# A graph attention layer on one core: the exponentials' transposes move from TensorE matmuls to VectorE 32x32 blocks and SBUF transfers, with attention three row blocks behind

## What is computed

```python
h = maximum(layernorm(x), 0)
q, k, v = h @ Wq + bq, h @ Wk + bk, h @ Wv + bv
adj = zeros((N, N)).at[src, dst].set(1.0)
a = q @ k.T / sqrt(512)
a = a * adj + (1 - adj) * -1e6
x = x + softmax(a, axis=-1) @ v
h = maximum(layernorm(x), 0)
agg = segment_sum(h[src], dst) / maximum(segment_sum(1, dst), 1)[:, None]
x = x + alpha * (agg @ W.T + b)
```

## Time and profile before

| what | value |
|---|---|
| median of three runs | 236.05 us |
| the profiled execution's own time | 235.76 us |
| its span in the profile | 233.9 us |
| TensorE busy | 230.2 us (98%) |
| VectorE busy | 161.5 us (69%) |
| ScalarE busy | 81.5 us (35%) |
| POOL busy | 76.0 us (32%) |
| granted TensorE clock | full speed (1.00) |

### The profile page before, as it was taken

One profiled execution on the slowest core, in us unless ns is written; L12 is line 12 of the kernel. 1 busy time (PEld: TensorE's weight loads), 2 busy tenths in 40 slices (PEclk: granted clock), 3 DMA queues, 4 the chain that ended last, 5 costly groups with the idle time before them and its releaser, 6 DMA issues.

```text
span 233.9 us, 3310 instructions
## 1 busy us (share of the span) xinstructions
PE 230.2 (98%) x1290; PEld 188.1 (80%) x1290; DVE 161.5 (69%) x282; ACT 81.5 (35%) x151; POOL 76.0 (32%) x106
## 2 busy tenths in 40 slices
PE   8999999999999999999999999999999999999995
PEld 6476788988888888888888888888888888888884
DVE  5998999999989755884759975757574262073222
ACT  3589927725114140431442341424242002060000
POOL 4386126510000059950702570706064206000000
PEclk9999999999999999999999999999999999999999
DMA  6999101000000020040000000000000000001232
GB/s 193 353 387 403 60 3 46 0 3 0 0 3 0 0 92 3 3 179 0 0 0 3 0 0 0 3 0 1 0 0 3 0 0 0 3 3 45 110 114 90
DMA packets 7152, 12.30 MB, mean 53 GB/s; under 512 B 1120, under 2 KB 2144, under 8 KB 7008
## 3 DMA queue, kind: packets, MB, share of 16 engines
q1 hardware_dynamic: 6272, 11.67, 13.8%
q10 hardware_dynamic: 864, 0.40, 0.6%
HBM read 9.97 MB, written 2.10 MB: 52 GB/s over the span
## 4 chain that ended last, share of the span: by engine, by line
PE 98%; DVE 0%; issue 0%; POOL 0%; DVEq 0%; POOLq 0%
PE bank L832 19%; PE bank L821 16%; PE bank L823 16%; PE bank L822 16%; PE bank L989 12%; PE bank L848 8%; PE bank L905 3%; PE bank L1009 3%; PE bank L898 3%; PE bank L882 1%; PE bank L816 1%; PE bank L892 1%; DVE o_sb L803 0%; PE bank L855 0%; PE bank L871 0%
## 5 line engine op out<-in xcount | busy, mean ns | idle before, releaser
L446 ACT ACTIVATE h2f<-xs,nmr,rstd 128x512 f32<-128x512 f32 x8 | 6.5, 816 | 56.1 <-POOL nmr L385 56.1
L821 PE MATMUL bank<-V_hi,pT_hi 128*128 128x512 f32 x64 | 25.5, 399 | 0.0
L577 DVE TENSOR_TENSOR ohW<-iotaW,key_b 128x1280 bf16<-128x1280 bf16 (+4 forms) x33 | 25.2, 764 | 0.0
L821 PE MATMUL bank<-hT_hi,GT_hi 128*128 128x512 f32 x64 | 25.1, 392 | 0.0
L573 DVE TENSOR_TENSOR ohL<-iotaL,lo_b 128x1024 bf16<-128x1024 bf16 x33 | 22.7, 687 | 3.5 <-PE bank L848 3.4
L823 PE MATMUL bank<-hT_hi,GT_lo 128*128 128x512 f32 x64 | 24.9, 390 | 0.0
L822 PE MATMUL bank<-V_lo,pT_hi 128*128 128x512 f32 x64 | 24.9, 390 | 0.0
L823 PE MATMUL bank<-V_hi,pT_lo 128*128 128x512 f32 x64 | 24.9, 390 | 0.0
L822 PE MATMUL bank<-hT_lo,GT_hi 128*128 128x512 f32 x64 | 24.9, 389 | 0.0
L989 PE MATMUL bank<-A,h_hi 128*128 128x512 f32 x64 | 24.9, 389 | 0.0
L989 PE MATMUL bank<-A,h_lo 128*128 128x512 f32 x64 | 24.9, 389 | 0.0
(11 more groups left out here) (133 smaller groups left out, 497.0 us busy)
## 6 DMA issues: line engine op xcount, KB each, us to landing
xs<-in_x SPq DMA_DIRECT2D x4, 512.0 KB, 8.0
out_dram<-o_sb SPq DMA_DIRECT2D x7, 256.0 KB, 2.0
wv_raw<-in_wv SPq DMA_DIRECT2D x1, 1024.0 KB, 11.4
wk_rows<-in_wk SPq DMA_DIRECT2D x1, 1024.0 KB, 12.8
wq_rows<-in_wq SPq DMA_DIRECT2D x1, 1024.0 KB, 11.7
wt_raw<-in_wT SPq DMA_DIRECT2D x1, 1024.0 KB, 5.1
wq_raw<-in_wqT SPq DMA_DIRECT2D x3, 256.0 KB, 7.7
wk_raw<-in_wkT SPq DMA_DIRECT2D x3, 256.0 KB, 7.6
```

The source lines that it names most:

```text
L577: nc.vector.tensor_tensor(ohW[:, q % RING, :, 0:row].rearrange("p b (m two) -> p b m two", two=2), bcast(iotaW[:, 0:row].rearrange("p (m t ...
L821: mm(out, lhs[0][a], rhs[0][b], start=(first and k == 0), stop=False)
```

## The change

- The 64 transposes on TensorE are gone. VectorE turns each of the 32 blocks of 32x32 of pr's row block in place in one instruction, `nc.vector.transpose`, into a new tile `turned` (128 x 1024). The block that stands in rows a and block column b then has to go to rows b: SP moves it with 16 transfers for each row block, each 32 partitions with 1 KB in each, from `turned` to `pT_f`. Both tiles have two buffers.
- pT_hi is one ScalarE copy of 1024 columns from pT_f in SBUF (it was two of 512 from PSUM), and pT_lo one VectorE subtraction of 1024 columns with both inputs in SBUF. Both walk quarter by quarter (`by_quarter`).
- The attention of a block, its residual, its second norm and POOL's work for it follow three row blocks behind the scores, not two. ScalarE's pT_hi and VectorE's pT_lo are for block i-2 in step i.
- POOL's fill waits for VectorE's transpose, not for TensorE's.
- wt lies where `turned` and `pT_f` lie, so SP loads it after the last pT_lo, and wt_hi and wt_lo are made in the last step (i = 10), no longer in i = 3; on VectorE `wt_lo` now stands ahead of the degrees and of the last residual.

The diff:

```diff
--- before.py
+++ after.py
@@ -196,8 +196,12 @@
         M = [place("M_hi", [P, KD, D], F32R, r_W2), place("M_lo", [P, KD, D], F32R, r_W2 + 8 * KB)]
 
         pr = [place(f"pr{i}", [P, N], F32, r_W0 + 4 * KB * i) for i in range(2)]
+        Q = 32
+        NQ = P // Q
+        pT_f = [place(f"pT_f{i}", [P, NQ, NT, Q], F32, r_W1 + (8 + 4 * i) * KB) for i in range(2)]
         pT = [[place(f"pT_hi{i}", [P, NT, P], F32R, r_W0 + (8 + 8 * i) * KB),
                place(f"pT_lo{i}", [P, NT, P], F32R, r_W0 + (12 + 8 * i) * KB)] for i in range(2)]
+        turned = [place(f"turned{i}", [P, NQ, NT, Q], F32, r_W1 + 4 * i * KB) for i in range(2)]
         h2f = [place(f"h2f{i}", [P, D], F32, r_W0 + (24 + 2 * i) * KB) for i in range(2)]
         r_st = [place(f"r_st{i}", [P, HALF], F32R, r_W0 + (24 + 2 * i) * KB) for i in range(2)]
         b_sb = place("b_sb", [P, D], F32, r_W0 + 28 * KB)
@@ -276,7 +280,8 @@
         gen_prep, gen_iota, gen_stage, gen_deg, gen_cols = (sem(n) for n in ("gen_prep", "gen_iota", "gen_stage", "gen_deg", "gen_cols"))
         agg_stage, agg_used = sem("agg_stage"), sem("agg_used")
         filled, scored, masked, maxed, expd = (sem(n) for n in ("filled", "scored", "masked", "maxed", "expd"))
-        pT_ps, pT_hi, pT_lo = sem("pT_ps"), sem("pT_hi"), sem("pT_lo")
+        blocks_turned, pT_hi, pT_lo = sem("blocks_turned"), sem("pT_hi"), sem("pT_lo")
+        pT_in = [sem(f"pT_in{i}") for i in range(2)]
         attended, x2_ready, h2_hi, h2_lo, res2_ready = (sem(n) for n in ("attended", "x2_ready", "h2_hi", "h2_lo", "res2_ready"))
         agg_ps, agg_hi, agg_lo = sem("agg_ps"), sem("agg_hi"), sem("agg_lo")
         rdeg_ready, out_ps, out_ready = sem("rdeg_ready"), sem("out_ps"), sem("out_ready")
@@ -288,6 +293,10 @@
         def bcast(ap, dim, n):
 
             return ap.unsqueeze(dim).broadcast_to([*ap.shape[:dim], n, *ap.shape[dim:]])
+
+        def by_quarter(tile):
+
+            return tile[:, :, :].rearrange("p t (b c) -> p b t c", b=NQ)
 
         def score_bank(i, q):
 
@@ -333,8 +342,15 @@
             sp.dma_start(bv_sb[:, :], bv_d.partition_broadcast(P)).then_inc(ld_bv, 16)
             sp.wait_ge(proj, NPROJ)
             sp.dma_start(b_sb[:, :], b_d.partition_broadcast(P)).then_inc(ld_b, 16)
-            sp.wait_ge(counts_final, 1)
-            sp.wait_ge(res_ready, NT)
+            for j in range(NT):
+                sp.wait_ge(blocks_turned, j + 1)
+                if j >= 2:
+                    sp.wait_ge(pT_lo, j - 1)
+                for a in range(NQ):
+                    for b in range(NQ):
+                        sp.dma_start(pT_f[j % 2][b * Q:(b + 1) * Q, a, :, :],
+                                     turned[j % 2][a * Q:(a + 1) * Q, b, :, :]).then_inc(pT_in[j % 2], 16)
+            sp.wait_ge(pT_lo, NT)
             sp.dma_start(wt_raw[:, :, :], wT_d.rearrange("(k p) n -> p k n", p=P)).then_inc(ld_wt, 16)
             for n, (j, cols) in enumerate(OUT):
                 sp.wait_ge(out_ready, n + 1)
@@ -403,7 +419,7 @@
             def fill(i):
 
                 if i >= 2:
-                    pool.wait_ge(pT_ps, 2 * (i - 1))
+                    pool.wait_ge(blocks_turned, i - 1)
                 else:
                     link(nc.gpsimd.memset(pr[i][:, :], 0.0))
                 nc.gpsimd.tensor_scalar(pr[i % 2][:, :], pr[i % 2][:, :], 0.0, negc[:, i:i + 1],
@@ -418,16 +434,16 @@
                 add_bv(t)
             pool.wait_ge(ld_b, 32)
             link(nc.gpsimd.tensor_scalar(b_sb[:, :], b_sb[:, :], alpha[:, :], None, ALU.mult))
-            for i in range(1, NT + 2):
+            for i in range(1, NT + 3):
                 if i + 1 < NT:
                     fill(i + 1)
-                if i >= 2:
-                    norm1(1, i - 2)
-
-                    pool.wait_ge(relu, NT + i - 1)
-                    link(nc.gpsimd.tensor_tensor(xs[:, i - 2, :], xs[:, i - 2, :], b_sb[:, :], ALU.add))
-                    nc.gpsimd.tensor_tensor(xs[:, i - 2, :], xs[:, i - 2, :], h2f[i % 2][:, :],
-                                            ALU.add).then_inc(res2_ready, 1)
+                if i >= 3:
+                    j = i - 3
+                    norm1(1, j)
+
+                    pool.wait_ge(relu, NT + j + 1)
+                    link(nc.gpsimd.tensor_tensor(xs[:, j, :], xs[:, j, :], b_sb[:, :], ALU.add))
+                    nc.gpsimd.tensor_tensor(xs[:, j, :], xs[:, j, :], h2f[j % 2][:, :], ALU.add).then_inc(res2_ready, 1)
 
 
         @block.scalar
@@ -497,25 +513,22 @@
                         act.wait_ge(dots, n + 1)
                         nc.scalar.activation(V[0][:, n, :], ps[:, :], ACT.Copy).then_inc(proj_hi, 1)
 
-            for i in range(NT + 2):
-                if 1 <= i <= NT:
-                    j = i - 1
+            for i in range(NT + 3):
+                if 2 <= i < NT + 2:
+                    j = i - 2
+                    act.wait_ge(pT_in[j % 2], 16 * NQ * NQ * (j // 2 + 1))
                     if j >= 2:
                         act.wait_ge(attended, j - 1)
-                    for q in range(2):
-                        act.wait_ge(pT_ps, 2 * j + q + 1)
-                        nc.scalar.activation(pT[j % 2][0][:, 4 * q:4 * q + 4, :],
-                                             bank[q][:, :].rearrange("p (b c) -> p b c", b=4),
-                                             ACT.Copy).then_inc(pT_hi, 1)
+                    nc.scalar.activation(by_quarter(pT[j % 2][0]), pT_f[j % 2][:, :, :, :], ACT.Copy).then_inc(pT_hi, 1)
                 if i < NT:
                     act.wait_ge(maxed, i + 1)
                     nc.scalar.activation(pr[i % 2][:, :], pr[i % 2][:, :], ACT.Exp, bias=negmax[:, i:i + 1],
                                          accum_out=rowsum[:, i:i + 1]).then_inc(expd, 1)
-                if i == 3:
+                if i == NT + 2:
                     act.wait_ge(ld_wt, 16)
                     nc.scalar.activation(wt[0][:, :, :], wt_raw[:, :, :], ACT.Copy).then_inc(w_hi, 1)
-                if i >= 2:
-                    j = i - 2
+                if i >= 3:
+                    j = i - 3
                     if j >= 2:
                         act.wait_ge(h2_lo, j - 1)
                         act.wait_ge(res2_ready, j - 1)
@@ -747,23 +760,25 @@
                         ins.then_inc(masked, 1)
                     dve.wait_ge(masked, 2 * i + 2)
                     nc.vector.tensor_reduce(negmax[:, i:i + 1], pr[i % 2][:, :], AX.X, ALU.max, negate=True).then_inc(maxed, 1)
-                if i == 3:
-                    dve.wait_ge(ld_wt, 16)
+                if 2 <= i < NT + 2:
+                    j = i - 2
+                    dve.wait_ge(pT_hi, j + 1)
+                    nc.vector.tensor_tensor(by_quarter(pT[j % 2][1]), pT_f[j % 2][:, :, :, :], f(by_quarter(pT[j % 2][0])),
+                                            ALU.subtract).then_inc(pT_lo, 1)
+                if i < NT:
+                    if i >= 2:
+                        dve.wait_ge(pT_in[i % 2], 16 * NQ * NQ * (i // 2))
+                    dve.wait_ge(expd, i + 1)
+                    nc.vector.transpose(turned[i % 2][:, :, :, :].rearrange("p b t c -> p t b c"),
+                                        pr[i % 2][:, :].rearrange("p (t b c) -> p t b c", t=NT, b=NQ)).then_inc(blocks_turned, 1)
+                if i >= 4:
+                    h2_lo_part(i - 4)
+                if i == NT + 2:
                     split_lo(3, wt, wt_raw)
-                if 1 <= i <= NT:
-                    j = i - 1
-                    for q in range(2):
-                        dve.wait_ge(pT_hi, 2 * j + q + 1)
-                        nc.vector.tensor_tensor(pT[j % 2][1][:, 4 * q:4 * q + 4, :],
-                                                bank[q][:, :].rearrange("p (b c) -> p b c", b=4),
-                                                f(pT[j % 2][0][:, 4 * q:4 * q + 4, :]), ALU.subtract).then_inc(pT_lo, 1)
+                    inverse_degrees()
                 if i >= 3:
-                    h2_lo_part(i - 3)
-                if i == NT + 1:
-                    inverse_degrees()
-                if i >= 2:
-
-                    j = i - 2
+
+                    j = i - 3
                     dve.wait_ge(expd, j + 1)
                     dve.wait_ge(res_ready, j + 1)
                     link(nc.vector.reciprocal(rinv[:, j:j + 1], rowsum[:, j:j + 1]))
@@ -992,32 +1007,19 @@
                         if h == NT - 1:
                             last.then_inc(agg_ps, 1)
 
-            for i in range(NT + 2):
-                if 2 <= i < NT:
+            for i in range(2, NT + 3):
+                if i < NT:
                     scores(i)
-                if 1 <= i <= NT:
-
-                    j = i - 1
-                    pe.wait_ge(expd, j + 1)
+                if i >= 3:
+                    j = i - 3
+                    pe.wait_ge(pT_lo, j + 1)
                     if j == 0:
                         pe.wait_ge(counts_final, 1)
```

(14 more changed lines are left out.)

## The result

| | before | changed |
|---|---|---|
| median | 235.98 us (235.86 to 236.27, 4 runs) | 246.37 us (245.38 to 247.15, 4 runs) |
| ratio | | 1.0436, 95% interval 1.0394 to 1.0478 |
| span of the profiled execution | 233.9 us | 245.3 us |
| TensorE busy | 230.2 us | 229.8 us |

The changed kernel is 4.4% slower, 10.4 us by the medians, and outside the predicted range. The profile's span has grown by 11.4 us. All ratios here compare mean times, so they can differ a little from the quotient of two medians.

The account below looks back on a forecast made before the run. TensorE's own work was taken as the bound: 7.0 us of transposes removed, 1.4 lost at the start and 2.6 at the end, net -3.0 us. That gave 233.0 us by the median, range 230.5 to 242.

Parts of the forecast that it names:

- What goes: 64 TensorE transposes in eight groups, all in the chain: removing them takes 7.0 us off, the whole possible gain.
- VectorE: In the steady attention stretch its work per row block becomes 9.5 to 10.1 us, fitting the 10.9 us period.
- the surcharge for meeting POOL: Each pT_lo on VectorE that meets a POOL instruction was taken to last 0.6 us longer.
- Rival 1: VectorE becomes the bound through a slower transpose, with 239.4 us at 2.0 us per transpose; chance 0.24.
- What SP gets: 16 issues per row block at a pitch of 0.44 us: 7.0 us, inside the 10.9 us period.
- rival 2: SP's issues or the transfers are the bound, costing from a pitch of 0.58; about 246 us at 0.7; chance 0.12.
- The landing: The last of a row block's transfers was taken to need 2.0 us to land.
- The end: Attention 6 waits 2.6 us for pT_lo; neighbour sums before attention 7 hide the last pT_lo and weight, costing nothing.
- Rival 3: TensorE's clock falls to 1.2 GHz behind both gaps, 243.7 us, or behind one, 238; chance 0.05.
- The two forecast waits: TensorE loses 1.4 us before block 0's attention and 2.6 us before block 6's.
- the signs that it named for being wrong: A wait before every attention, VectorE waiting for pT_hi mid-stretch, an SP queue never resting, or a clock under 1.00.

Follow-up runs that it names:

- the last experiment: Changed kernel with the move through DRAM, later wait for the last pT_lo, reordered VectorE and ScalarE, and wt_lo behind the last residual: 229.08 us.
- half_issues: Changed kernel with 8 transfers of 32 x 2 KB per row block instead of 16 of 32 x 1 KB, omitting the move between row groups: 235.82 us.
- no_transfers: Changed kernel with no SBUF transfers; pT_hi and pT_lo read the tile VectorE turned, omitting the move between row groups: 236.21 us.
- sixteen_stores: Changed kernel moving each row block by 16 stores to DRAM and four loads, with the last pT_lo wait behind the neighbour sums: 245.40 us.
- late_wait: Changed kernel with TensorE's wait for the last pT_lo put back behind the 48 neighbour-sum matmuls: 241.81 us.
- issues_ordered: Changed kernel with its 16 transfers, later last pT_lo wait, degree sums of blocks 0 and 1 later, block 6's pT_hi and pT_lo earlier: 243.05 us.
- filled_waits: Changed kernel with throwaway matmuls in TensorE's waits before attentions 0 and 6 and before the neighbour sums: 244.83 us.
- two_queues_late: Changed kernel with 8 of each block's 16 transfers issued by ScalarE, and the last pT_lo wait behind the neighbour sums: 248.59 us.
- via_dram_late: Changed kernel moving each row block by one store to DRAM and four loads, with the last pT_lo wait behind the neighbour sums: 234.25 us.

## Why the prediction was wrong

**What goes: right.** 7.0 us of transposes could be had, and the last experiment has them, 7.3 by its medians.

**VectorE: right.** The transpose was taken at 1.2 us of engine time and has 1.17; pT_lo was taken at 1.2 and has 1.22 alone, pT_hi 1.06. Only the surcharge for meeting POOL was low: 0.6 was taken, and pT_lo takes up to 1.95 in the changed kernel and up to 2.19 in half_issues. Even so VectorE fits: in no_transfers it is busy 9.9 us of a 10.9 us period (142.9 to 153.8 us). The estimate by eight times the Trainium skill's 311 ns ("VectorE: DVE Perf Modes", "The three transpose paths") would have been 2.49: the trace sides with one instruction of 1.25 us for all 1024 columns. Rival 1 did not occur.

**What SP gets: wrong, and this is the step that failed.** "I take a pitch of 0.44: 7.0 us for 16, inside the period of 10.9." It is 0.655, or 10.5 us for 16. The issues of the earlier trace rows all have DRAM at one end, and that it would be the same from SBUF to SBUF was assumed; sixteen_stores has 0.42 for such transfers even in this shape, where 0.59 is the price from SBUF to SBUF. The test itself was wrong too: 10.5 us is still "inside the period of 10.9", so by it nothing would have been late. What counts is the whole row of issues. SP starts at block 0's transpose, near 96, and has 7 x 16 issues to make before block 6's data are there; TensorE comes to block 6's attention early, because at the end attentions follow each other every 5.45 us without scores between them. That the transfers are small, the argument against rival 2, was beside the point, since the price does not hang on size. The landing, 2.0 us, was right (1.9). Block 0's data are late already: ScalarE starts on them at 108.59, where 104.7 was forecast, and the first wait is 3.1 us. Rival 2 had the mechanism and the point from which it costs, 0.58, but only 0.12 of the chance. By its own formula block 6's data land at 95.7 + 7 x 16 x 0.655 + 2.0 = 171.1 us; ScalarE starts on them at 171.33. That is 8.1 us after the 163.0 at which it would have asked, and about 241 us. late_wait, which has this loss and not the next, took 241.81. The rest up to 246 is in the next step, the clock's part of it in the one after.

**The end: wrong in one place.** "The 48 neighbour-sum matmuls (10.88 us, rows 2) come before attention 7 and hide pT_lo of block 7." They don't: the diff puts `pe.wait_ge(pT_lo, j + 1)` ahead of them for the last block too, where the kernel before waited behind them. I read the order of the matmuls and not that of the waits. With late transfers this costs 4.6 us (late_wait), the half-clock stretch behind it included; without them still 1.2 (half_issues).

**The clock: underrated.** Rival 3 had 0.05 on stretches of 1.2 GHz behind the gaps. Three of the four gaps had one. It cost less than the 5.45 us for each gap of the prediction, 1.5 to 1.9 us in all, since a stretch lost 1.7 and only the last stood in the chain; but behind a forecast wait of 2.6 us it belonged in the sum: half_issues and no_transfers each have one behind their wait of 2.5.

**The two forecast waits: right.** 1.4 and 2.6 were forecast; with the transfers out of the way they are 0.9 and 2.5 (no_transfers), and they go when the order is changed.

So even at SP's pitch as predicted the kernel would very likely have been no faster: with 1.2 us and 1.7 us more than forecast, half_issues, whose issues take less still, is a draw. The prediction of 3.0 us gained was wrong by one large term and two small ones, all of the same sign. Of the signs that it named for being wrong, two are in the profile: an SP queue that never rests, and a clock under 1.00. Four experiments missed their expected times (sixteen_stores by 1.4 us, issues_ordered by 0.2 beyond its 1 us), two of them in a way that teaches: filled_waits (241.3 expected, 244.83 measured) added up losses of which only one was in the chain, and two_queues_late priced the issues on ScalarE's queue but not what stands behind them.

**Open.** Whether attention three blocks behind is needed, or two would do with the faster move, was not tried. Why an issue from SBUF to SBUF costs more was not looked into.

## What to carry to other kernels

Count the DMA issues of a queue as work with a price each, and take the price from a transfer with the same two ends: here 0.59 us from SBUF to SBUF, whatever the bytes, against 0.34 to 0.43 with DRAM at one end. Their number matters more than the price: five transfers by way of DRAM beat sixteen direct ones by 7.6 us (234.25 against 241.81), but sixteen stores and four loads by the same way took 245.40. Then add up the whole row of issues and compare its end with when the data are asked for; a row that fits in each period can still be late. When a diff moves a wait, write down what stands behind it on that engine; here one line, moved up by 48 matmuls, cost 4.6 us. A cause that is hidden behind a longer chain is worth nothing until that chain is cut: the same two moves in the order gained 3.8 us with the fast move and nothing with the slow one.

## What the runs showed of the hardware that was not expected

- An issue from SBUF to SBUF takes 0.59 us on SP's queue and 0.61 on ScalarE's, for 32 x 1 KB, 32 x 2 KB and 128 x 1 KB (0.60) alike; 32 x 1 KB to DRAM takes 0.42. The two queues pay it side by side.
- In the changed kernel gaps of 3.0 to 5.2 us on TensorE were followed by a stretch in which eight matmuls took 3.4 us, half speed; a gap of 1.3 us by none. The length alone does not decide it: behind half_issues' gap of 2.5 us (the profile's count) the granted clock was 0.64 in the next 3.2 us, behind late_wait's of 2.55 before attention 0 it stayed 1.00, and one of via_dram_late's four executions had no drop. After the changed kernel's first gap (work again from 110.96) the granted clock was 0.91 from 110 to 113 us and 0.52 from 113 to 116, so the drop came only after matmuls had run again for more than a microsecond.
- A VectorE transpose of 32x32 blocks over 128 x 1024 float32 takes 1.25 us, the same as a row maximum over that width (1.22).
- A subtraction on VectorE with both inputs in SBUF goes from 1.22 us to 1.95 (changed kernel) and 2.19 (half_issues) beside POOL's work. The Trainium skill has the rule ("SBUF — State Buffer", "SBUF: two separate sides"): against a POOL instruction that reads SBUF, the one that starts second waits until the other ends. The trace agrees in kind: in half_issues one started at 163.65, while POOL's addition ran to 164.73, and took 2.15 us, where the full wait and 1.22 would be 2.30.
